# A 3x3 convolution moved to TensorE, and attention blocks turned two squares at a time

## The reference

```python
qkv = jnp.einsum('oi,bihw->bohw', qkv_w, xh)             # xh: layer-normed half, 32 channels
q, k, v = jnp.split(qkv, 3, axis=1)
lepe = jax.lax.conv_general_dilated(v, lepe_w, (1, 1), 'SAME', feature_group_count=c)   # 3x3, per channel
attn = jnp.einsum('nhqc,nhkc->nhqk', q * scale, k) + bias[None]     # 4x4 squares, 8 heads of 4 channels
attn = jax.nn.softmax(attn, axis=-1)
out = jnp.einsum('nhqk,nhkc->nhqc', attn, v) + lepe
...
x = x + conv(layernorm_over_channels(x))                 # sum of the plain and the rolled result
t = t + ffn(layernorm(t))                                # softmax router, top 2 of 8 experts, 64x64 each
```

## Time and profile before

| | |
|---|---|
| time, median of 3 runs | 3483.31 us (3472.05 to 3487.70) |
| profiled execution, first to last instruction | 3495.3 us |
| busy: PE, DVE, POOL, ACT | 3038.4, 3088.6, 2932.3, 2038.3 us (87, 88, 84, 58%) |
| mean granted TensorE clock | 0.925 |
| DMA engines, hardware and software queues | 36.3% and 13.5% of their time |

### The profile page before, as it was taken

One profiled execution on the slowest core, in us unless ns is written; L12 is line 12 of the kernel. 1 busy time (PEld: TensorE's weight loads), 2 busy tenths in 40 slices (PEclk: granted clock), 3 DMA queues, 4 the chain that ended last, 5 costly groups with the idle time before them and its releaser, 6 DMA issues.

```text
span 3495.3 us, 200950 instructions
## 1 busy us (share of the span) xinstructions
PE 3038.4 (87%) x82372; PEld 1892.0 (54%) x82372; DVE 3088.6 (88%) x6049; ACT 2038.3 (58%) x4130; POOL 2932.3 (84%) x5382
## 2 busy tenths in 40 slices
PE   5889888888898888998888988889899899889886
PEld 3655555555555555555555555555555555555551
DVE  3789999889999888998999889999899899999995
ACT  3666666556565556665666656566556656666651
POOL 5998888888898788987888878889788988888970
PEclk8999999999899899998999989999899989999986
DMA  2345555545555455545555544555455555555555
GB/s 58 85 122 147 137 143 138 143 130 143 136 144 139 125 144 137 145 130 133 136 139 140 139 131 130 143 135 143 130 140 138 143 134 145 137 143 137 138 124 151
DMA packets 427432, 469.79 MB, mean 134 GB/s; under 512 B 117616, under 2 KB 407920, under 8 KB 426480
## 3 DMA queue, kind: packets, MB, share of 16 engines
q1 hardware_dynamic: 260592, 342.97, 36.3%
q0 software_dynamic: 165888, 113.57, 13.5%
HBM read 264.97 MB, written 77.86 MB: 98 GB/s over the span
## 4 chain that ended last, share of the span: by engine, by line
PE 36%; DVE 22%; issue 14%; DMA 12%; SPq 9%; POOL 3%; ACT 3%; DVEq 1%; ACTq 0%; POOLq 0%
PE bank L585 9%; PE bank L652 8%; SPq L454 6%; DMA gate_wide<-gate_rows 6%; DVE lepe L896 6%; DMA z<-fin 5%; PE bank L570 5%; DVE row_max L904 3%; PE bank L658 2%; PE bank L612 2%; POOL vx L528 2%; PE bank L624 2%; DVE probT L969 2%; SPq L449 1%; DVE gx L884 1%
## 5 line engine op out<-in xcount | busy, mean ns | idle before, releaser
L528 POOL DMA_DIRECT2D vx<-vt x3072 | 1555.5, 515 | 201.9 <-PE bank L658 181.0
L652 PEld LDWEIGHTS bank<-probT,vx 128*32 128x32 f32 x36864 | 825.8, 188 | 442.4 <-issue 378.2
L652 PE MATMUL bank<-probT,vx 128*32 128x16 f32 x36864 | 888.2, 234 | 170.7 <-issue 117.5
L516 POOL DMA_DIRECT2D kx<-k_sb x1536 | 738.8, 488 | 230.9 <-issue 114.6
L585 PEld LDWEIGHTS bank<-kx,qx 32*32 32x32 f32 x36864 | 602.9, 112 | 434.9 <-issue 432.2
L585 PE MATMUL bank<-kx,qx 32*32 32x64 f32 x36864 | 709.9, 227 | 128.5 <-issue 90.9
L742 ACT ACTIVATE prob<-prob 128x512 f32<-128x512 f32 x576 | 367.4, 638 | 538.9 <-DVE prob L909 538.6
L896 DVE SCALAR_TENSOR_TENSOR lepe<-vpad,table,lepe 128x384 f32<-128x384 f32 x960 | 630.8, 657 | 0.0
L884 DVE TENSOR_TENSOR gx<-gate_wide,yn_pair 128x768 f32<-128x768 f32 x384 | 393.8, 1026 | 194.4 <-DMA gate_wide<-gate_rows 148.0
L547 POOL TENSOR_TENSOR lepe_p<-lepe_p,tap_sb 128x384 f32<-128x384 f32 x384 | 435.0, 1133 | 39.0 <-issue 18.5
L904 DVE TENSOR_REDUCE row_max<-bank 128x32 f32<-128x512 f32 x576 | 394.4, 685 | 29.5 <-PE bank L585 16.4
(11 more groups left out here) (75 smaller groups left out, 3801.9 us busy)
## 6 DMA issues: line engine op xcount, KB each, us to landing
gate_wide<-gate_rows SPq DMA_DIRECT2D x768, 192.0 KB
vx<-vt POOLq DMA_DIRECT2D x3072, 12.0 KB
kx<-k_sb POOLq DMA_DIRECT2D x1536, 24.0 KB
z<-fin SPq DMA_DIRECT2D x192, 192.0 KB, 4.3
yn_pair<-yn POOLq DMA_DIRECT2D x384, 96.0 KB
xa<-in_x SPq DMA_DIRECT2D x192, 96.0 KB, 3.3
xn<-xa SPq DMA_DIRECT2D x192, 96.0 KB
xs<-xn SPq DMA_DIRECT2D x96, 192.0 KB
```

The lines of the kernel that those rows point to most:

```text
L516: pool.dma_start(kx[to + m:to + C:4, r % 2, m, :], k_sb[at + m:at + C:4, r % 2, :])\
L528: pool.dma_start(vx[to:to + TOK, r % 2, col:col + 13:4, odd, :], vt[at:at + TOK, r % 2, x::2, :, :].rearrange("p h n k -> p h (n k)"))\
L652: last = MM(bank_o[32 * c:32 * c + 32, at * TOK:(at + 1) * TOK], vx[:, kr % 2, :, at % 2, at // 2 * 4 + ba], probT[:, kr % 2, at, ba * TOK ...
```

## The change

- **The convolution goes to PE.** v is linear in the layer-normed x, so the 3 x 3 taps and the v weights are multiplied into one matrix per tap beforehand (`conv_w`, made by DVE at the start). SP loads 10 rows of the normed x per tile into `halo` (partitions 64 to 127 hold the same, one row down, so that two taps stand in one matmul). PE makes 12 matmuls of 128 rows x 64 columns per tile, 4 in each of three slots (3 sides, 2 groups of taps, 2 half rows), and sums the plain and the rolled convolution. All taps on DVE, ACT and POOL go, with `vpad`, `lepe`, `att` and PE's second v (L615).
- **Tiles are 64 channels x two half rows** instead of 64 channels x two strips. `x_tile` and the output are laid out for that outside the kernel; `load_tile` has 5 DMAs, the output 1. `y` is now the sum of the convolution in PSUM, x, `z0t` and `z2t`, in three adds (`y_first`, `y_second`, `y_third`).
- **The blocks that are turned** hold one head of two squares half a row apart instead of two heads of one square. `score` writes its 64 columns in four runs of 16, `product` writes 4 x 4 columns in place, the row sums are 8 matmuls of 192 columns instead of 4 of 384, and v is placed by 8 DMAs of 24 KB per strip instead of 16 of 12 KB.
- `fin` is now the division itself, one slot earlier. The gates' bank is needed for the convolution: logits and gates go through `bank_p[1]` with waits of `query_key` and `router` for them, `logits` moves from slot 0 to slot 2, the gates are turned by one transpose instead of three, and the experts' bias is three matmuls of 128 columns instead of one of 384.

```diff
-    tap_products=15, pool_taps=16, taps=19, add_taps=24,
-    store_z=24, load_tile=33, y_first=37, y_second=38, tile_sum=39, tile_variance=40, router=41, logits=42,
-    take_logits=43, gates=45, gap_exp=46, turn_gates=47, pair_yn=47, store_gates=48, spread_gates=49,
+    store_z=24, load_halo=29, load_tile=33, conv=34, y_first=37, y_second=38, y_third=38, tile_sum=39, tile_variance=40, router=41, logits=44,
+    take_logits=44, gates=45, gap_exp=46, turn_gates=47, pair_yn=47, store_gates=48, spread_gates=49,
...
-                    MM(bank_p[1][:, 0:SPX], wo, xs[:, r % 4, :], start=True, stop=True).then_inc(vo_made, 1)
+                if (ti := s.in_tile("conv")) and ti[2] < len(SIDES):
+                    k, r, side = ti
+                    t, dw = (r + 1) % IMT, SIDES[side]
+                    if side == 0:
+                        pe.wait_ge(halo_loaded[r % 2], halos_to(s, r) * 16)
+                        if s.later(r, 1):
+                            pe.wait_ge(y_step, k * 2 - 1)
+                    first = [side == 0, side == 0]
+                    for group, skip in ((0, 0), (1, 2)):
+                        for top, end, which in conv_rows(t)[group]:
+                            for y_ in range(2):
+                                low, high = y_ * HALFW + max(0, -dw - y_), (y_ + 1) * HALFW - max(0, dw + y_ - 1)
+                                last = MM(by_rows(bank_c[y_ * C:(y_ + 1) * C, 0:SPX], HALFW)
+                                          [:, top:end, low - y_ * HALFW:high - y_ * HALFW],
+                                          conv_w[:, which, group * 3 + side, :],
+                                          by_rows(halo[:, r % 2, :], W)[:, top + skip:end + skip, low + dw:high + dw],
+                                          start=first[y_], stop=(side == 2 and group == 1), skip_group_check=True)
+                                first[y_] = False
+                    if side == 2:
+                        last.then_inc(conv_made, 1)
-                            last = MM(bank_o[32 * c:32 * c + 32, at * TOK:(at + 1) * TOK],
+                                last = MM(out_window(bank_o[32 * m:32 * m + 32, cols], n), vx[:, kr % 2, :, n, m * 2 + a],
...
-                            pe.wait_ge(picked, k)
+                            pe.wait_ge(fin_made, k)
...
-                        for x in range(2):
-                            for odd in range(2):
...
+                        for y_ in range(2):
+                            at, col = g * CH + y_ * TOK, y_ * TOK + g * HD
+                            pool.dma_start(vx[at:at + TOK, r % 2, col:col + HD, :, :].rearrange("p h n k -> p (h n k)"),
+                                           vt[at:at + TOK, r % 2, :, :, :].rearrange("p h n k -> p (h n k)"))\
+                                .then_inc(v_spread[r % 2], 16)
-                        G.tensor_tensor(lepe_p[:, kr % 2, :], lepe_p[:, kr % 2, :], tap_sb[:, j - 1, :],
-                                        ALU.add).then_inc(pool_lepe_made, 1)
...
-                    V.tensor_tensor(att[:, r % 2, :], bank_o[:, 0:SPX], row_inv[:, r % 2, :], ALU.mult).then_inc(picked, 1)
+                    V.tensor_tensor(fin[:, r % 2, :], bank_o[:, 0:SPX], row_inv[:, r % 2, :], ALU.mult).then_inc(fin_made, 1)
-                    V.tensor_tensor(y[:, r % 4, :], xt[:, r % 2, :], z0t[:, r % 2, :], ALU.add).then_inc(y_step, 1)
+                    dve.wait_ge(conv_made, k + 1)
+                    V.tensor_tensor(y[:, r % 4, :], bank_c[:, 0:SPX], xt[:, r % 2, :], ALU.add).then_inc(y_step, 1)
...
+                if yt := s.tile("y_third"):
...
+                    V.tensor_tensor(y[:, r % 4, :], y[:, r % 4, :], z2t[:, r % 2, :], ALU.add).then_inc(y_made, 1)
-                if taps:
-                    tap(taps[0], taps[1], 2 * taps[2])
```

More of the change, by code:

```diff
@@ L48 @@
 UNITS = WIN // UW
+PAIRED = WIN // 2
+UPAIR = UW // 2
+HALFW = W // 2
 UPX = UW * TOK
@@ L206, in lay_tables @@
         rows = slice(g * CH, (g + 1) * CH)
-        for h in range(HD):
-            for m in range(HEADS):
-                a, b, y = m // 4, m // 2 % 2, m % 2
+        for place in range(HEADS):
+            a, m = place // 4, place % 4
+            head = (place - roll * ROLL) % HEADS
+            for h in range(HD):
                 for part, name in ((0, "wq"), (1, "wk")):
-                    put(name, rows, g * CH + a * 16 + h * 4 + m % 4, qkv_w[part * CH + h * HEADS + m])
-                here = (h - 1) % HD if roll and a and b else h
-                one = qkv_w[2 * CH + here * HEADS + m]
-                put("wv", rows, g * CH + h * 8 + y * 4 + b * 2 + a, one)
-                at = (a * 2 + b) * CH + roll * 16 + h * 4 + half * 2 + y
-                put("wo", rows, at, one)
-                put("taps", at, slice(0, 9), lepe_w[here * HEADS + m].reshape(9))
@@ L219, in lay_tables @@
-    for g in range(4):
-        for a in range(2):
+                    put(name, rows, g * CH + a * 16 + h * 4 + m, qkv_w[part * CH + h * HEADS + head])
+                own = (h * HEADS + place - roll * ROLL) % CH
+                put("wv", rows, g * CH + h * HEADS + m * 2 + a, qkv_w[2 * CH + own])
             for i in range(TOK):
-                for m in range(4):
+                for y in range(2):
                     for j in range(TOK):
                         dr, dw = i // SP - j // SP + SP - 1, i % SP - j % SP + SP - 1
-                        put("bias", g * CH + a * TOK + i, m * TOK + j, bias_table[dr * (2 * SP - 1) + dw, a * 4 + m])
+                        put("bias", g * CH + a * TOK + i, (m * 2 + y) * TOK + j, bias_table[dr * (2 * SP - 1) + dw, head])
@@ L226, in lay_tables @@
     order = tile_channels()
+    for col, channel in enumerate(order):
+        half, o = channel // CH, channel % CH
+        for roll, name in ((0, "plain"), (ROLL, "rolled")):
+            own = (o - roll) % CH
+            for i in range(CH):
+                for copy in range(2):
+                    put("v_" + name, copy * C + (half * CH + i + roll) % C, col, qkv_w[2 * CH + own, i])
+            taps = lepe_w[own].reshape(3, 3)
+            for side in range(3):
+                dw = SIDES[side] + 1
+                put("taps_" + name, slice(0, C), side * C + col, taps[0, dw])
+                put("taps_" + name, slice(C, 128), side * C + col, taps[1, dw])
+                put("taps_" + name, slice(0, C), (3 + side) * C + col, taps[2, dw])
@@ L231, in lay_tables @@
             put("experts", rows, slice(p * C, (p + 1) * C), expert_w[2 * p + half][np.ix_(order, order)])
-        put("expert_bias", slice(half * E, (half + 1) * E), slice(half * C, (half + 1) * C), expert_b[:, order])
+        for blk in range(TBLK):
+            at = blk * GE + half * E
+            put("expert_bias", slice(at, at + E), slice(blk * 128 + half * C, blk * 128 + (half + 1) * C),
+                expert_b[:, order])
         put("router_bias", slice(half * E, (half + 1) * E), 0, router_b)
@@ L458, in put_rolled @@
-                    def put_rolled(half, at, row, rows):
-                        put_z(z2t, half, 1, 1, 0, 3, at, row, rows)
-                        put_z(z2t, half, 1, 0, 3, 1, at, row, rows)
-                    for half in range(2):
-                        put_x(half)
-                        put_z(z0t, half, 0, 0, 0, 4, 0, t * (2 * SP) + half * SP, SP)
-                    put_rolled(0, 0, (t * (2 * SP) + H - ROLL) % H, ROLL)
-                    put_rolled(0, ROLL, t * (2 * SP), SP - ROLL)
@@ L491, in slot @@
                     im = bass.ds(s.image(r, IMT), 1)
-                    for half in range(2):
-                        sp.dma_start(out_flat[im][:, :, (t * (2 * SP) + half * SP) * W:(t * (2 * SP) + half * SP + SP) * W]
-                                     .rearrange("b c n -> c (b n)"), y_out[half * C:(half + 1) * C, r % 2, :])\
-                            .then_inc(out_stored[r % 2], 16)
+                    sp.dma_start(out[im][:, t].rearrange("b p n -> p (b n)"), y_out[:, r % 2, :])\
+                        .then_inc(out_stored[r % 2], 16)
             pipeline(sp, slot)
             for p in range(2):
-                sp.wait_ge(out_stored[p], N_TILE // 2 * 32)
+                sp.wait_ge(out_stored[p], N_TILE // 2 * 16)
         @block.gpsimd
```

295 lines of the change are left out of this document (157 added, 138 removed).

## The result

The changed kernel takes 3646.7 us (median of 4 runs, 3641.3 to 3661.8), the kernel before, on the same chip, 3485.5. The ratio is 1.0473, with a 95% interval from 1.0445 to 1.0501: 4.7% slower, where 2.6% faster was forecast.

The account below looks back on a forecast made before the run. With DVE and POOL relieved, PE was taken as the bound: 32.2 us work, 1.6 idle and 0.8 clock make 34.6 a tile against 35.3. With 25 us gained early that gave 3395 us, range 3285 to 3475.

Parts of the forecast that it names:

- What PE still waits for: PE's idle time per tile after the change: 1.6 us stay of 4.0, bounds 0 to 2.5.
- The other waits go: PE's waits outside slot 3 vanish, since DVE at 23.5 us a tile is ahead in the other slots.
- DVE's lateness: Before the change, DVE comes late to `y_out` in slot 2, 0.9 us after the expert pair's end, so PE waits.
- PE's round trip: From expert pair to `tile_sum`: PE's own steps take 6.5 us, the other engines' chain 8.1, leaving 1.6 idle.
- The clock: Cost of PE's time at the lower clock falls from 1.9 to 0.8 us a tile as idle time shrinks.
- The rival with the clock: Clock falls as often as now after slot 3's idle piece, costing 1.9 us a tile; 3495 or 3530 us; chance 0.09.
- DVE and POOL: Busy time per tile after relief: DVE from 32.1 to about 23.5 us, POOL from 30.5 to 17.8.
- PE's work: PE's matmul time per tile at the higher clock: about 29.4 us plus 2.8, so 32.2.
- the third rival: The convolution's 24 weight loads on PE are not hidden: 3.3 us more, 37.9 us a tile, 3685 us; chance 0.05.
- `tile_sum`'s stall: In slot 3, PE waits for ACT's copy of k: 1.80 us in the trace before, 1.6 a tile forecast.
- The early stretch: From 45 to 200 us, before the experts, POOL's halved load makes PE the limit; worth about 25 us.
- the chain behind it: Steps from `y_out` through DVE's slot 2 to `tile_sum`: 7.48 us before, 7.2 forecast after.

Follow-up runs that it names:

- b_no_taps: The kernel before with its taps on POOL, ACT and DVE left out, PE's instructions unchanged; 3320.2 us, ratio 0.952.
- v_quiet_tile: The whole change with halo loaded in slot 1, convolution in slots 2 to 4, x and z loads one slot later; 3396.4 us, ratio 0.973.

## Why the prediction was wrong

- **The step that failed** is "What PE still waits for": idle time from 4.0 to 1.6 us a tile, "The other waits go". It stayed at 3.9. I had read the whole idle time as DVE's lateness and PE's round trip. By the table, only 2.1 us of it were waits; they fell to 0.9, below the 1.6 that was to stay. The other 2.0 were PE at the end of its instructions, pauses and late starts, which the prediction has no term for, and these grew to 3.0 in the change, where the transfers crowd in slots 5 and 0. Two rows of PE's waits that end with issue stood in the trace of before; I passed over them:
```profile
PE bank L652 <- issue: 117.5, 140, 2.0
PE bank L585 <- issue: 90.9, 63, 4.0
```
- **The clock** followed that step: 1.9 to 0.8 was forecast. PE spent 4.7 us a tile at 1.2 GHz before and 5.6 after; at half price that is a cost of 2.3 and 2.8. The rival with the clock had the sign; its stall was `tile_sum`'s, while most of the idle time came with late instructions.
- **DMA had no place in the sum.** The halo was costed at nothing. Without it the change is 109 us faster; given to the kernel before, it costs 55 us.
- **DVE and POOL:** right. DVE per tile went to 2080.89 / 89.9 = 23.1 us (forecast 23.5), POOL to 17.3 (17.8); a DMA of 24 KB costs POOL 486 ns, one of 12 KB 515.
- **PE's work:** mis-sized to the safe side. Less idle time and half of the time at the lower clock, a tile's work goes from 35.4 - 4.0 - 2.3 = 29.1 to 37.0 - 3.9 - 2.8 = 30.3 us, +1.2 instead of +2.8. The convolution is right at 1.46 for 1.44 us a group, and its loads are hidden, so the third rival falls (its sum, by the way, gives 3693 us and not 3685). The products with the new patterns are not slower but 0.3 us shorter each, six times a tile; what makes them so was not tested.
- **`tile_sum`'s stall:** still on ACT's copy of k, but 53.9 us in all, 0.6 us a tile, not 1.6. The 1.80 us of the earlier trace rows were one tile and no typical one: the row of the whole profile before has 0.6 us a tile too. In b_no_taps it nearly goes, so the chain behind it was read rightly, but it was the smaller part of PE's idle time:
```profile
PE bank L672 <- ACT k_sb L765: 61.0, 69, 2.1
```
- **The early stretch** gave nothing: tile 10's first score starts at 376 us, 17 us later than before (359).
- v_quiet_tile lands within 2 us of the forecast, with other terms: idle 2.6 us a tile instead of 1.6, work 34.2 - 2.6 - 0.8 = 30.8 instead of 32.2. That is luck in the sum, not a proof of it.

## What to carry to other kernels

Idle time in the middle of equal matmuls, put down to issue, was no engine's lateness here: look at the instruction queue's packets and at what the data queues moved ahead of them, and count instructions per microsecond where TensorE runs many small matmuls. A transfer that nobody waits for can still cost time, and a wait in an in-order queue can decide which transfers meet; before a change that adds bytes is given up, move its loads, and move the same loads in the kernel before, or the change is credited with what the order gave.

## What was unexpected of the hardware

- TensorE's instructions come in packets of 16 KB, 703 of them, by a queue (q8) that the profile lists with the data queues of the 16 DMA engines. 480 KB of data a tile more, unused, raised the pauses from 1.5 to 2.3 us a tile.
- Less work for TensorE can mean a lower clock: with one convolution group of three, 7.4 us a tile were spent at 1.2 GHz instead of 5.6.
- Four convolution matmuls with eight weight loads, into the two column halves, step 1.46 us, and products that write their 16 columns as 4 x 4 in place step 0.99 us where those of before took 1.29.
